# A two-layer graph network on one core: first loads on three queues, transposed score blocks in batch 0, wider score pieces, new instruction orders

## The chip, the cores and the metric

The kernel runs on one core of a Trainium2 chip. The core has five engines with an instruction queue each: TensorE (PE; its weight loads are listed as PEld), VectorE (DVE), ScalarE (ACT), GpSimd (POOL) and SyncE (SP), which here only starts transfers. Each engine runs its own instructions in their written order and waits for others at semaphores. SP, ACT and POOL can start DMAs. The metric is the device time of one execution in microseconds, the median of several.

## The reference

For each of 8 batches (x is 1024 x 128, adj 1024 x 1024 of zeros and ones), with EPS terms left out:

```python
def layer0(x, adj):                       # attention over the graph
    u = x @ x.T / sqrt(128)
    delta = softmax(u, -1) * adj
    att = delta / (delta.sum(-1) + 1e-10)
    ctx = triu(att, 1) @ (x @ Wl.T + bl) + diag(att) * (x @ Ws.T + bs) + tril(att, -1) @ (x @ Wr.T + br)
    return relu(ln_w * normed(ctx) + ln_b)

def layer1(x, adj):                       # graph convolution
    d = (adj.sum(-1) + 1e-5) ** -0.5
    return (d[:, None] * adj * d[None, :]) @ (x @ weight) + bias

x = layernorm(x + layer0(x, adj))
x = layernorm(x + layer1(x, adj))
```

## The kernel before

All work is in blocks of 128 rows; NB = 8 block rows a batch (called rows here), HB = 4 is half of them. The batches run one into the other: while batch b starts, the layer-1 products of batch b-1 (called p in the code) are still running. Nothing is scheduled by a tool at run time: for each engine the functions `first_batches`, `batch` and `last_batches` write out, call by call, the order of its work. The steps of a batch are:

- **x.** `load_x` brings all 8 rows of x; TensorE transposes them for batches 0 and 1 (`turn_x`), later ones are transposed by VectorE in 32 x 32 blocks and DMAs (`turn_rows`, `move_rows`). ScalarE writes the high part (`x_high`), VectorE the low part (`x_low`) of a split-precision product. `split_matmul` (L435) is three matmuls for one product.
- **Projections.** `project` multiplies one row by the three weights (384 columns) into the PSUM bank `ps_m`, and VectorE's `add_bias` moves it out. The orders place `m_read_h` ahead of the next projection, a wait until it has been moved.
- **Scores.** `scores(b, i)` makes 128 x 1024 scores of row i. Since x x' is symmetric, in batches 1 to 7 only the blocks from the diagonal on are multiplied, in one piece up to column 512 and one behind it; the blocks before the diagonal are transposed (L483) from copies that ScalarE made of earlier rows (`keep`, L841, into `kept`). In batch 0 (`halves(b)`) each row is multiplied in full, with rows 1 and 3 in the bank `ps_c`.
- **Softmax and mask.** VectorE's `row_max`, ScalarE's `exps`, VectorE's `masked` (times adjacency, with a sum).
- **Context.** TensorE turns the row (`turn_d`, 8 transposes), ScalarE moves it (`d_out`), GpSimd makes three masked copies of the diagonal block (`masks`), TensorE multiplies (`context_far`, `context_near`).
- **Norms.** `add_self`, `stats_c` (VectorE), `scale_c` (GpSimd: a power and a product), `norm_c` (ScalarE), `affine`, `stats_x`, `scale_x`, `norm_x`.
- **Layer 1.** The adjacency is transposed by VectorE (`turn_blocks`) and 16 DMAs for each half (`move_blocks`). `gather(b, i0, i1, j0, j1)` sums over source rows j for target rows i0 to i1; it waits until all of the group of rows that holds j1-1 have been normalised (`group_end`: rows 0 to 3, and in the last batch 4, 5 and 6, 7). `y_out` moves it out, `second_product` multiplies by the weight, `add_out` adds, `stats_f`, `scale_f` and `norm_f` normalise, `store` writes.

In the last batch the target rows are taken in three groups: 0 to 3, 4 to 6, and 7. Its normalisation is VectorE's, and all stores are on SP:

```python
            for i in range(i0, i1):                                   # norm_f_on, L286
                v = fin[:, i, :]
                last = eng.tensor_scalar(v, v, power["f"][:, i:i + 1], shift["f"][:, i:i + 1], ALU.mult, ALU.add)
```

Before the first transposes TensorE multiplies zeros (`first_products`), which VectorE writes into 512 columns first. The first loads all stand on SP: x, three weights, three biases broadcast to all partitions, then adjacency rows. Other engines' places that the text speaks of are the beginning and the end of each list.

## Time and profile before

| | us |
|---|---|
| three runs | 442.7, 443.6, 443.77 (median 443.6) |
| the profiled execution | 445.5 |
| its span, first to last instruction | 443.8 |
| TensorE busy | 431.7 (97%) |
| VectorE busy | 381.1 (86%) |
| ScalarE busy | 318.7 (72%) |
| GpSimd busy | 302.2 (68%) |

The engines' busy time says who is close to its limit over the whole; a busy time by stage says where. In the timeline, two starts on TensorE in a row tell the price of the first instruction better than its listed length, because matmuls overlap. A bracket behind a row gives the engine's idle time before it and what ended it.

### The profile page before, as it was taken

The numbers are of one execution on the slowest core, as the hardware profiler recorded it, in microseconds if no ns is written. First come the engines' busy times: TensorE is split into PE (matmuls) and PEld (weight loads), VectorE is DVE, ScalarE is ACT, GpSimd is POOL, SyncE is SP. The second block draws the span as 40 slices with busy tenths as digits, with TensorE's granted clock in tenths as the row PEclk, the third lists the DMA queues.
The fourth block names the chain that finished last, engine by engine and source line by source line (L and its number), as shares of the span: only waits on it lengthen the run. The fifth ranks groups of instructions, "written<-read, shape, count | busy, mean of one in ns | idle before, by whom it ended". The sixth has DMA issues, their size and how long they took to land. (4 is left out here: it accounts for less than half of the span.)

```text
span 443.8 us, 9076 instructions
## 1 busy us (share of the span) xinstructions
PE 431.7 (97%) x2775; PEld 355.7 (80%) x2775; DVE 381.1 (86%) x699; ACT 318.7 (72%) x674; POOL 302.2 (68%) x364
## 2 busy tenths in 40 slices
PE   7999999999999999999999999999999999999984
PEld 4789989779787888869887797977987789897743
DVE  2899898997999889997999989999799988998536
ACT  2588887778677787678876787677777777887420
POOL 2034666668777778758796687766877596897882
PEclk9999999999999999999999999999999999999998
DMA  5925859489765885468943888538866589254801
GB/s 163 350 68 146 264 162 258 143 214 257 151 185 136 246 244 136 153 168 280 220 141 111 204 273 216 178 110 216 267 137 189 142 245 273 55 132 98 199 19 54
DMA packets 68880, 79.91 MB, mean 180 GB/s; under 512 B 7232, under 2 KB 60608, under 8 KB 68832
## 3 DMA queue, kind: packets, MB, share of 16 engines
q1 hardware_dynamic: 68768, 79.26, 65.3%
q8 instruction: 23, 0.38, 0.4%
q14 instruction: 25, 0.20, 0.1%
q0 software_dynamic: 64, 0.07, 0.1%
HBM read 38.40 MB, written 4.19 MB: 96 GB/s over the span
## 5 line engine op out<-in xcount | busy, mean ns | idle before, releaser
L1481 POOL TENSOR_TENSOR dM<-dT,parts 128x384 f32<-128x384 f32 x64 | 72.5, 1132 | 67.4 <-ACT dT L851 54.9
L517 PE MATMUL ps_c<-h_sum,dT 128*128 128x128 f32 x896 | 110.4, 275 | 0.0
L517 PEld LDWEIGHTS ps_c<-h_sum,dT 128*128 128x128 f32 x896 | 106.4, 192 | 2.9 <-issue 2.5
L537 PE MATMUL ps_y<-aT,x1p 128*128 128x512 f32 x224 | 106.3, 593 | 0.0
L838 ACT ACTIVATE d_rows<-ps_u,nmax 128x1024 f32<-128x1024 f32 x62 | 68.8, 1110 | 49.4 <-DVE nmax L1124 49.3
L1124 DVE TENSOR_REDUCE nmax<-ps_u 128x1 f32<-128x1024 f32 x62 | 75.2, 1213 | 18.9 <-PE ps_u L483 16.9
L1131 DVE CUSTOM_DVE_ANT_0 d_rows<-d_rows,a_rows 128x1024 f32<-128x1024 f32 x64 | 83.7, 1315 | 0.3
L851 ACT ACTIVATE dT<-ps_d 128x1024 f32<-128x1024 f32 x64 | 65.4, 1022 | 25.7 <-PE ps_d L502 23.4
L1138 DVE STREAM_TRANSPOSE a_blk<-a_rows 128x1024 f32<-128x1024 f32 x64 | 77.7, 1228 | 0.0
L857 ACT ACTIVATE junk<-a_rows 128x1024 fp8e4<-128x1024 f32 x64 | 67.2, 1049 | 0.3
L502 PEld LDWEIGHTS ps_d<-parts,d_rows 128*128 128x128 f32 x512 | 58.9, 140 | 10.5 <-issue 9.8
L502 PE MATMUL ps_d<-parts,d_rows 128*128 128x128 f32 x512 | 66.3, 273 | 0.5 <-ACT dT L851 0.5
L537 PEld LDWEIGHTS ps_y<-aT,x1p 128*128 128x128 f32 x224 | 38.4, 191 | 24.4 <-issue 24.4
L437 PE MATMUL ps_u<-xT_hi 128*128 128x512 f32 (+3 forms) x96 | 43.1, 449 | 0.0
L298 DVE TENSOR_TENSOR h_sum<-ps_m,bias_bc 128x384 f32<-128x384 f32 x64 | 35.3, 552 | 6.9 <-PE ps_m L439 5.6
L523 PE MATMUL ps_c<-h_sum,dM 128*128 128x128 f32 x256 | 39.0, 275 | 0.0
L523 PEld LDWEIGHTS ps_c<-h_sum,dM 128*128 128x128 f32 x256 | 34.7, 191 | 3.3 <-issue 1.7
L438 PE MATMUL ps_u<-xT_lo,xT_hi 128*128 128x512 f32 (+3 forms) x96 | 34.0, 354 | 0.0
L439 PE MATMUL ps_u<-xT_hi,xT_lo 128*128 128x512 f32 (+3 forms) x96 | 33.9, 353 | 0.0
L1550 POOL TENSOR_TENSOR power_f<-var_f,minus_half 128x4 f32<-128x4 f32 (+2 forms) x17 | 21.9, 1290 | 17.3 <-DVE nmean_f L1237 14.8
L437 PE MATMUL ps_m<-wT_hi,xT_hi 128*128 128x384 f32 x64 | 29.5, 461 | 1.3 <-DVE h_sum L298 0.9
L872 ACT ACTIVATE c_rows<-c_rows,shift_c,power_c 128x128 f32<-128x128 f32 x64 | 26.3, 483 | 5.1 <-POOL shift_c L1501 5.1
(104 smaller groups left out, 751.6 us busy)
## 6 DMA issues: line engine op xcount, KB each, us to landing
a_rows<-in_adj_dram SPq DMA_DIRECT2D x64, 512.0 KB, 4.6
aT<-a_blk SPq DMA_DIRECT2D x224, 128.0 KB, 3.2
x_rows<-in_x_dram SPq DMA_DIRECT2D x8, 512.0 KB, 3.9
a_rows<-a_blk SPq DMA_DIRECT2D x32, 128.0 KB, 2.4
out_dram<-fin SPq DMA_DIRECT2D x15, 256.0 KB, 2.6
x_turned<-x_blk SPq DMA_DIRECT2D x96, 32.0 KB, 1.9
out_dram<-fin SPq DMA_DIRECT2D x1, 192.0 KB, 2.1
fin<-in_L_gnn_Wl_dram SPq DMA_DIRECT2D x1, 64.0 KB, 3.6
```

What stands on the lines that cost most here:

```text
L437: pe.matmul(o, hi_l, hi_r, start=True, stop=False)
L502: last = pe.transpose(ps_d[:, j, :], d_rows[:, g % 3, j * P:(j + 1) * P], ident)
L517: pe.matmul(ps_c[:, c_place(b, i), :], dT[:, i % 2, j, :], h_sum[:, b % 2, j, k * H:(k + 1) * H], start=t == 0, stop=False)
L523: last = pe.matmul(ps_c[:, c_place(b, i), :], dM[:, i % 2, k, :], h_sum[:, b % 2, i, k * H:(k + 1) * H], start=False, stop=k == 1)
L537: last = pe.matmul(y_bank(b, i0, i1), gathered(b)[:, j, :], turned(b)[:, i0:i1, :, j, :].rearrange("p i q c -> p (i q) c"), start=j == 0, ...
L838: act.activation(d_rows[:, g % 3, :], u_bank(b, i), ACT.Exp, bias=nmax[:, i % 2:i % 2 + 1], accum_out=zsum[:, i:i + 1]).then_inc(exp_done, 1)
L851: act.activation(dT[:, i % 2, :, :], ps_d[:, :, :], ACT.Copy).then_inc(dt_out, 1)
L857: act.activation(junk[:, :], a_rows[:, i, :], ACT.Copy, accum_out=deg[:, i:i + 1], saturate=False)\
L1124: dve.tensor_reduce(nmax[:, i % 2:i % 2 + 1], u_bank(b, i), AX.X, ALU.max, negate=True)\
L1131: dve.tensor_tensor_reduce(out=d_rows[:, g % 3, :], in0=d_rows[:, g % 3, :], in1=a_rows[:, i, :], scale=1.0, scalar=0.0, op0=ALU.mult, op1 ...
L1138: dve.transpose(a_blk[:, i, :, :, :], a_rows[:, i, :].rearrange("p (j m c) -> p m j c", m=NQ, c=Q))\
L1481: pool.tensor_tensor(dM[:, i % 2, :, :], dT[:, i % 2, i, :].rearrange("p (a c) -> p a c", a=1).to_broadcast([P, 3, P]), parts[:, :, :], AL ...
```

## The change

- `load_x_half`: batch 0's x comes in two loads with a semaphore each; the weights are loaded from ScalarE's queue, the biases and the norm constants from GpSimd's. GpSimd makes the identity first, and TensorE's start waits for it alone.
- The zeros are 128 columns, and the second warm-up product is 256 wide for 384.
- In batch 0, rows 0 to 3 are multiplied in full, the first half as soon as the first half of x is there; ScalarE keeps their right halves. Rows 4 to 7 are made as in the other batches, with transposes of kept blocks.
- `first_column`: rows 3 and 7 (from batch 1 on; row 7 in batch 0 too) multiply from one block further left, so that their short piece is 256 wide for 128, with one transpose less. Row 6 is not kept any more.
- Batch 0's odd projections go to the bank `ps_y`.
- The last normalisation subtracts the mean and multiplies by the power, without a shift, except where ScalarE does it: rows 0 to 6 of the last batch, whose rows 4 to 6 ScalarE also stores.
- All orders are new. In the last batch several gathers are cut into smaller steps.

```diff
+        def h_bank(b, j):
+            return (ps_y if b == 0 and j % 2 else ps_m)[:, 0:3 * H]
-        def halves(b):
-            return b == 0
+        def halves(b, i):
+            return b == 0 and i < HB
         def kept_before(b, i):
-            return (NB - 1) * (b - 1) + i
+            return (NB - 2) * b + min(i, NB - 2)
+        def first_column(i):
+            return i - (i % HB == HB - 1)
...
-            eng.wait_ge(f_scale, NB * b + i1)
+            eng.wait_ge(f_power, NB * b + i1)
             for i in range(i0, i1):
                 v = fin[:, i, :]
-                last = eng.tensor_scalar(v, v, power["f"][:, i:i + 1], shift["f"][:, i:i + 1], ALU.mult, ALU.add)
+                mean = f_stats_of(i, 1) if b == B - 1 and i >= NB - 2 else stats["f"][:, i, 1:2]
+                last = eng.tensor_scalar(v, v, mean, power["f"][:, i:i + 1], ALU.subtract, ALU.mult)
...
+            def load_x_half(b, half):
+                sp.dma_start(x_rows[:, b, blocks_of(half), :], x_block_rows(x, b, HALF * half, HALF * (half + 1)))\
+                  .then_inc(x_in[b] if half else x0_in, 16)
...
             def first_batches(b, p):
-                load_x(p)
-                load_weights()
-                load_biases()
+                load_x_half(p, 0)
+                load_x_half(p, 1)
                 load_a(p, 0)
-                load_a(p, 3)
                 load_a(p, 1)
...
-                for c in (slice(0, HALF), slice(HALF, HALF + 3 * P)):
-                    pe.matmul(ps_u[:, c], d_rows[:, 0, 0:P], d_rows[:, 0, 0:c.stop - c.start], start=True, stop=True)
+                zero = d_rows[:, 0, 0:P]
+                for n in (HB, 2):
+                    pe.matmul(ps_u[:, 0:n * P], zero, zero.rearrange("p (a c) -> p a c", a=1).to_broadcast([P, n, P]),
+                              start=True, stop=True)
...
             def scores(b, i):
-                pe.wait_ge(xt_split, 2 * (b + 1))
+                if b or i >= HB:
+                    pe.wait_ge(xt_split, 2 * (b + 1))
...
-                j0 = 0 if halves(b) else i
+                j0 = 0 if halves(b, i) else first_column(i)
                 for c in (slice(j0 * P, HALF), slice(max(j0 * P, HALF), N)):
+                    if b == 0 and i < HB:
+                        pe.wait_ge(xt_split, 2 if c.start else 1)
...
             def keep(b, i):
                 act.wait_ge(nmax_ready, NB * b + i + 1)
-                for v, j0, j1 in kept_parts(i):
-                    last = act.activation(v, ps_u[:, j0 * P:j1 * P].rearrange("p (j c) -> p j c", c=P), ACT.Copy)
+                for v, j0, j1 in kept_parts(i) if b or i else [(kept[:, 1, :, :], HB, NB)]:
+                    if b == 0 and j1 <= HB:
+                        continue
+                    last = act.activation(v, u_bank(b, i)[:, j0 * P:j1 * P].rearrange("p (j c) -> p j c", c=P), ACT.Copy)
...
-                gather(b, 0, HB, 0, HB)
-                gather(b, HB, NB - 1, 0, HB)
-                gather(b, NB - 1, NB, 0, 2)
-                gather(b, 0, HB, HB, NB)
+                gather(b, 0, HB, 0, 3)
+                gather(b, HB, NB - 1, 0, 1)
+                gather(b, 0, HB, 3, HB)
+                gather(b, HB, NB - 1, 1, HB)
+                gather(b, 0, HB, HB, NB - 2)
+                gather(b, 0, HB, NB - 2, NB)
```

VectorE's first instructions before (`nmax` is a row's maximum, `h_sum` a projection with its bias, `ISA d_rows,dsum` the masked product, `wT_lo` the low part of the weights):

```order
L1102 MEMSET d_rows 128x512
L1114 SCALAR_TENSOR_TENSOR xT_lo<-ps_m,xT_hi 128x512
L1106 SCALAR_TENSOR_TENSOR wT_lo<-ps_d,wT_hi 128x384
L1114 SCALAR_TENSOR_TENSOR xT_lo<-ps_y,xT_hi 128x512
L298 TENSOR_TENSOR h_sum<-ps_m,bias_bc 128x384
L1124 TENSOR_REDUCE nmax<-ps_u 128x1
L298 TENSOR_TENSOR h_sum<-ps_m,bias_bc 128x384
L1124 TENSOR_REDUCE nmax<-ps_c 128x1
L298 TENSOR_TENSOR h_sum<-ps_m,bias_bc 128x384
L1131 ISA d_rows,dsum<-d_rows,a_rows 128x1024
L1131 ISA dsum 128x1
```

and now:

```order
L1141 MEMSET d_rows 128x128
L1153 SCALAR_TENSOR_TENSOR xT_lo<-ps_m,xT_hi 128x512
L1153 SCALAR_TENSOR_TENSOR xT_lo<-ps_y,xT_hi 128x512
L1177 STREAM_TRANSPOSE a_blk<-a_rows 128x1024
L1163 TENSOR_REDUCE nmax<-ps_u 128x1
L1145 SCALAR_TENSOR_TENSOR wT_lo<-ps_d,wT_hi 128x384
L1163 TENSOR_REDUCE nmax<-ps_c 128x1
L311 TENSOR_TENSOR h_sum<-ps_m,bias_bc 128x384
L1170 ISA d_rows,dsum<-d_rows,a_rows 128x1024
L1170 ISA dsum 128x1
```

The first projection's bias has moved behind the maxima of rows 0 and 1, and block row 0 of the adjacency (`a_blk`) is turned ahead of them all.

TensorE's last instructions before, after the last context product (`ps_y` are the gathers for target rows 0 to 3, `ps_u` with 384 columns rows 4 to 6, with 128 row 7; `ps_m` and `ps_d` the second products):

```order
L537 MATMUL ps_y<-a_rows,h_sum 128x512 x4
L537 MATMUL ps_u<-a_rows,h_sum 128x384 x4
L537 MATMUL ps_u<-a_rows,h_sum 128x128 x2
L537 MATMUL ps_y<-a_rows,h_sum 128x512 x4
L537 MATMUL ps_u<-a_rows,h_sum 128x384 x2
L549 MATMUL ps_m<-w_sb,yT 128x128 x4
L537 MATMUL ps_u<-a_rows,h_sum 128x384 x2
L537 MATMUL ps_u<-a_rows,h_sum 128x128 x3
L549 MATMUL ps_d<-w_sb,kept 128x128 x3
L537 MATMUL ps_u<-a_rows,h_sum 128x128 x3
L549 MATMUL ps_d<-w_sb,kept 128x128
```

and now:

```order
L550 MATMUL ps_y<-a_rows,h_sum 128x512 x3
L550 MATMUL ps_u<-a_rows,h_sum 128x384
L550 MATMUL ps_y<-a_rows,h_sum 128x512
L550 MATMUL ps_u<-a_rows,h_sum 128x384 x3
L550 MATMUL ps_y<-a_rows,h_sum 128x512 x4
L550 MATMUL ps_u<-a_rows,h_sum 128x384 x2
L562 MATMUL ps_m<-w_sb,yT 128x128 x4
L550 MATMUL ps_u<-a_rows,h_sum 128x384 x2
L550 MATMUL ps_u<-a_rows,h_sum 128x128 x3
L562 MATMUL ps_d<-w_sb,kept 128x128 x3
L550 MATMUL ps_u<-a_rows,h_sum 128x128 x5
L562 MATMUL ps_d<-w_sb,kept 128x128
```

The gather into `ps_y` is cut after three, one and four steps (the four are two calls with a wait of their own each), and row 7's gather has moved behind the others.

VectorE's very last instructions before, from the sum of row 7 on:

```order
L1213 SCALAR_TENSOR_TENSOR fin<-ps_d,dinv,h_sum 128x128
L290 TENSOR_SCALAR fin<-fin,power_f,shift_f 128x128 x4
L1225 BN_STATS stats_odd<-fin 128x6
L1234 TENSOR_SCALAR var_f<-stats_odd 128x1
L1237 TENSOR_SCALAR nmean_f<-stats_odd 128x1
L290 TENSOR_SCALAR fin<-fin,power_f,shift_f 128x128 x4
```

and now:

```order
L1252 SCALAR_TENSOR_TENSOR fin<-ps_d,dinv,h_sum 128x128
L1264 BN_STATS stats_odd<-fin 128x6
L1273 TENSOR_SCALAR var_f<-stats_odd 128x1
L303 TENSOR_SCALAR fin<-fin,stats_odd,power_f 128x128
```

Seven normalisations have left VectorE's list, four of them from between the sum of row 7 and its statistics.

## Rows read from the trace of the kernel before

**Rows 1.** Busy time of each engine in one stage, its columns named above.

```profile
core 0: us, PE busy (x) PEld busy (x) DVE busy (x) ACT busy (x) POOL busy (x), PEclk, DMA share, GB/s
350.00:400.00 50.00, 50.00 (x349) 43.38 (x348) 45.46 (x84) 39.31 (x82) 39.64 (x45) 1.00 0.70 181
```

**Rows 2.** The timeline of the start: start, length, engine, line, what, [idle before].

```profile
1.51 3.35 PE L455 MATMUL ps_u<-d_rows 128*128 128x512 f32 x4 [1.51 <-DVE d_rows L1102]
...
4.27 4.93 SPq L315 DMA_DIRECT2D a_rows<-in_adj_dram  x6
...
4.81 1.09 PE L460 MATMUL ps_m<-parts,x_rows 128*128 128x128 f32 x4
...
6.56 0.69 DVE L1114 SCALAR_TENSOR_TENSOR xT_lo<-ps_m,xT_hi 128x512 fp32r<-128x512 f32 x1 [5.10 <-ACT xT_hi L830]
...
10.98 0.40 PE L439 MATMUL ps_u<-xT_hi,xT_lo 128*128 128x512 f32 x1
...
26.06 0.39 PE L437 MATMUL ps_u<-xT_hi 128*128 128x512 f32 x1
```

**Rows 3.** First 45 us: x's loads, their landing; then the adjacency loads' landing.

```profile
L308 SPq DMA_DIRECT2D x_rows<-in_x_dram x2: 441/552/664, 0.8 to 9.2; - x2
...
DMA to landing us min/median/max: 3.9/7.6/11.4
...
DMA to landing us min/median/max: 3.3/9.2/11.9
```

**Rows 4.** TensorE's timeline, a projection and row 2's scores of one batch.

```profile
109.11 0.33 PE L439 MATMUL ps_m<-wT_hi,xT_lo 128*128 128x384 f32 x1
109.28 0.28 PE L437 MATMUL ps_u<-xT_hi 128*128 128x256 f32 x1
...
109.64 0.40 PE L437 MATMUL ps_u<-xT_hi 128*128 128x512 f32 x1
109.87 0.40 PE L438 MATMUL ps_u<-xT_lo,xT_hi 128*128 128x512 f32 x1
```

**Rows 5.** TensorE's timeline, row 7's scores of one batch and what follows.

```profile
89.27 0.28 PE L438 MATMUL ps_u<-xT_lo,xT_hi 128*128 128x128 f32 x1
...
89.49 0.95 PE L483 MATMUL ps_u<-parts,kept 128*128 128x128 f32 x7
...
90.28 1.88 PE L537 MATMUL ps_y<-aT,x1p 128*128 128x512 f32 x4
```

**Rows 6.** Busy time from row 0's to row 4's maximum; then VectorE and ScalarE rows.

```profile
12.11:24.38 12.27, 11.09 (x58) 8.86 (x56) 11.60 (x17) 7.71 (x12) 1.78 (x1) 1.00 0.76 284
...
24.76 1.23 DVE L1138 STREAM_TRANSPOSE a_blk<-a_rows 128x1024 f32<-128x1024 f32 x1
...
95.33 1.64 ACT L872 ACTIVATE c_rows<-c_rows,shift_c,power_c 128x128 f32<-128x128 f32 x4
...
98.11 1.22 DVE L1124 TENSOR_REDUCE nmax<-ps_u 128x1 f32<-128x1024 f32 x1
...
100.00 1.11 ACT L838 ACTIVATE d_rows<-ps_u,nmax 128x1024 f32<-128x1024 f32 x1
...
101.09 0.92 ACT L844 ACTIVATE kept<-ps_u 128x896 f32<-128x896 f32 x1
```

**Rows 7.** The timeline of the end, all engines.

```profile
424.25 0.88 ACT L872 ACTIVATE h_sum<-c_rows,shift_x,scale_x 128x128 f32<-128x128 f32 x2 [2.09 <-POOL shift_x L1529]
...
427.54 3.67 PE L537 MATMUL ps_y<-a_rows,h_sum 128*128 128x512 f32 x8 [1.48 <-ACT h_sum L872]
...
437.29 0.49 PE L549 MATMUL ps_d<-w_sb,kept 128*128 128x128 f32 x2 [0.37 <-ACT kept L893]
...
438.26 0.34 DVE L1213 SCALAR_TENSOR_TENSOR fin<-ps_d,dinv,h_sum 128x128 f32<-128x128 f32 x1
438.51 1.13 DVE L290 TENSOR_SCALAR fin<-fin,power_f,shift_f 128x128 f32<-128x128 f32 x4
...
440.25 0.79 POOL L1550 TENSOR_TENSOR power_f<-var_f,minus_half 128x1 f32<-128x1 f32 x1 [0.69 <-DVE var_f L1234]
...
441.34 0.35 DVE L290 TENSOR_SCALAR fin<-fin,power_f,shift_f 128x128 f32<-128x128 f32 x1 [0.34 <-POOL shift_f L1554]
```

More of the change, by code:

```diff
@@ L273, in squares, with scaled_by_act @@
             return stats[norm][:, blk, 2]
+        def scaled_by_act(b, i1):
+            return b == B - 1 and i1 < NB
         def f_stats_of(i, t):
@@ L376, in first_batches, with batch @@
                 load_a(b, 0)
-                load_norm_constants()
+                load_a(b, 2)
+                move_blocks(p, 0)
+                load_a(b, 1)
+                load_a(b, 4)
+                move_blocks(p, 1)
+                load_a(b, 3)
+                load_a(b + 1, 0)
+                load_a(b, 7)
+                load_x(b + 1)
+                load_a(b, 6)
+                load_a(b, 5)
+                move_rows(b)
+            def batch(b, p):
                 load_a(b, 1)
@@ L379, in first_batches, with last_batches @@
                 move_blocks(p, 0)
+                load_a(b, 4)
+                load_a(b, 7)
+                load_a(b, 2)
+                move_blocks(p, 1)
+                store(p - 1, 0, HB)
+                load_a(b + 1, 0)
+                store(p - 1, HB, NB)
+                load_a(b, 3)
+                load_x(b + 1)
                 load_a(b, 6)
+                load_a(b, 5)
+                move_rows(b)
+            def last_batches(b, p):
                 load_a(b, 2)
+                load_a(b, 3)
+                load_a(b, 1)
+                move_blocks(p, 0)
+                load_a(b, 5)
+                load_a(b, 7)
+                store(p - 1, 0, HB)
@@ L490, in project @@
                     pe.wait_ge(const_ok, 1)
+                if b == 0 and j % 2:
+                    pe.wait_ge(xt_split, 2)
+                    wait(pe, h_added, j - 1)
                 s = slice(j * P, (j + 1) * P)
-                split_matmul(ps_m[:, 0:3 * H], xT_hi[:, b % 2, s], xT_lo[:, b % 2, s], wT_hi[:, :], wT_lo[:, :])\
+                split_matmul(h_bank(b, j), xT_hi[:, b % 2, s], xT_lo[:, b % 2, s], wT_hi[:, :], wT_lo[:, :])\
                     .then_inc(h_ready, 1)
@@ L817, in _, with load_weights @@
         def _(act):
+            def load_weights():
+                for k, w in enumerate((Wl, Wr, Ws)):
+                    act.dma_start(wraw[:, k, :], w).then_inc(const_in, 16)
             def weights():
@@ L886, in norm_x, with norm_f, store @@
                 normalize(gathered(b), c_rows, "x", i0, i1).then_inc(x1p_ready, i1 - i0)
+            def norm_f(b, i0, i1):
+                act.wait_ge(f_scale, i1)
+                act.wait_ge(f_norm, NB * b + i0)
+                normalize(fin, fin, "f", i0, i1).then_inc(f_norm, i1 - i0)
+            def store(b, i0, i1):
+                act.wait_ge(f_norm, NB * b + i1)
+                act.dma_start(x_block_rows(out, b, i0 * P, i1 * P), fin[:, i0:i1, :]).then_inc(fin_free[i0 // HB], 16)
             def y_out(b, i0, i1):
@@ L1088, in last_batches @@
                 y_out(b, NB - 1, NB)
+                norm_f(b, 0, HB)
+                norm_f(b, HB, NB - 1)
+                store(b, HB, NB - 1)
+            load_weights()
             first_batches(1, 0)
@@ L1380, in last_batches, with batch @@
+                row_max(b, 7)
+                masked(b, 6)
+                x_low(b + 1, 0)
+                stats_c(b, 0, HB)
+                stats_f(p, 0, HB)
+            def batch(b, p):
                 x_low(b, 1)
```

670 lines of the change are left out of this document (320 added, 350 removed).

## The prediction

> **What bounds the kernel now.** I read the busy time by stage first. In the stage from 350 us to 400 us TensorE is busy for all of the 50 us, VectorE for 45.5 (91%), ScalarE and GpSimd for 39 [rows 1]; the seven stages before it, back to 30 us, read alike for TensorE and VectorE. TensorE's starts follow one another without a hole there, so it is the bound in the middle, and a new order can take nothing from it: only less TensorE work can. Two other places are left. One is the start: work on TensorE begins at 4.81 us, and it limps until about 25 us [rows 2]. The other is the end: a wait of 1.48 us at 427.54 us, and 4 us of small steps behind the last matmul (start 437.29, end 437.78) [rows 7].
>
> To measure the start I use lost time: the moment at which an instruction starts, less the TensorE work that stands ahead of it at full rate. The full-rate steps from start to start are: a 512-wide split-precision matmul 0.23 us, a 384-wide one 0.17, a 256-wide one 0.12 (three from 109.28 to 109.64) [rows 4]; a 128-wide one 0.11 (two from 89.27 to 89.49), a 128x128 transpose 0.11 (seven from 89.49 to 90.28; I use 0.109) [rows 5]. Row 5's scores of batch 0 start at 26.06. Ahead of them stand 11 transposes (1.20), five rows of scores of six 512-wide matmuls (6.96), 8 projections of three 384-wide (4.16) and 3 turned rows of 8 transposes (2.62): 14.9 us. Lost so far: 11.1 us.
>
> **1. Less TensorE work.** Batch 0, rows 4 to 7: 24 wide matmuls become three 512-wide, three 384-wide and six 256-wide, with 21 transposes of kept blocks. That is -21 x 0.232 + 3 x 0.174 + 6 x 0.118 + 21 x 0.109 = -4.87 + 0.52 + 0.71 + 2.29 = -1.35 us. Rows 3 and 7 of batches 1 to 7: 42 matmuls go from 128 to 256 columns, at 0.12 for 0.11, +0.25 us; 14 transposes fall away, -1.53 us. Together **-2.6 us**, all on the path, since TensorE has no hole to hide it. Doubling the columns costs next to nothing only because the 128-wide product is as slow as the 256-wide one [rows 4, 5]. If the new 256-wide ones were priced by their width against the 128-wide, 42 x 0.11 = 4.6 us would come on top and the term would be +1.8; the row at 109.28 is the same operation in the same place, so I keep 0.12. ScalarE copies more for batch 0 (eight copies at most 0.9 us each [rows 6]) and less for every other batch; it is the emptier engine, and I take nothing for it beyond the chain below.
>
> **2. The start.** The warm-up products last 3.35 us, four passes of two products, at the lower rate [rows 2]. The second shrinks from 384 to 256 columns: 3.35 x 768/896 = 2.9, or less; and VectorE's memset is a quarter as wide, 0.3 us sooner. They end near 4.0 instead of 4.86; the memset's gain is my estimate, from 0.5 us that it can at most give. The first half of x is 256 KB; the whole landed 3.9 us after its issue at 0.8, at 4.7 [rows 3], so the half lands between 2.8 (half of 3.9 after the issue) and 4.7; I take 3.8. TensorE begins at 4.0. Eight transposes at 0.21 (1.09 for four [rows 2], the lower rate) end at 5.7. ScalarE's and VectorE's share of the first half ended 1.35 us after such transposes (5.90, then 6.56 + 0.69 = 7.25 [rows 2]); the first four end at 4.9, so the first half is there at 6.3 and the second, VectorE's 0.69 later, at 7.1. The six matmuls of row 0 run at the lower rate, 0.46 each: 6.3 to 9.0. Row 0's maximum starts at 9.0, where it started at 12.11 (the left end of the stretch in [rows 6]).
>
> From there VectorE's own queue is the chain up to row 4's maximum. Before, it was busy for 11.60 of the 12.27 us of this stretch, with five maxima, five bias additions and three masked products [rows 6]. The new order has the same between these points and one turned block row (1.23 [rows 6]) and the low part of the weights (at most the 0.69 of the wider one; I take 0.6) more. With 0.7 us of idle time, since row 1's scores come late, that is 14.1 us, and row 4's maximum ends at 23.1. Its exponentials (1.2) and kept copies (0.5) [rows 6] release row 5 at 24.8; the copies are new on this path. TensorE has by then 15.1 us of work behind it (four full rows 5.57, row 4 at 1.14, 15 transposes 1.64, projections 4.16, turned rows 2.62). Lost: 9.7 instead of 11.1, **-1.4 us**. The cover has to hold: after this point row 6's exponentials and copies have a context product of 3.5 us before them, and none of the later pairs is closer than 3.4 us of TensorE work.
>
> VectorE turns block row 0 before row 0's maximum, so it must have adjacency row 0 by 7.8 us. The issue was the eighth on SP, at 4.27 us [rows 2], the first at 0.8 [rows 3]: 0.5 us each. It is now the third, at 1.8. Loads of that kind took from 3.3 to 11.9 us [rows 3], the late ones behind others in line. In its own queue it has only x ahead of it now, so it should be nearer to x's own 3.9 than to the median of 9.2: I take 6 us, 7.8, just in time. At both ends it costs nothing or 2 us and more. The Trainium skill, page DMA: Bandwidth & Descriptors, section Issuing engines are not separate DMA queues, says that loads started on several engines still share the same 16 DMA engines and that only the issue time is saved; by that rule the three queues bring the 2.4 us of issue and no faster landing. No row here separates the two.
>
> **3. The end.** The wait at 427.54 is for the last two normalised rows, while rows 4 and 5 are ready since 425.13 (424.25 + 0.88) and the 512-wide gather asks for all four at once. Split, its two steps for rows 4 and 5 (2 x 0.86 us; eight passes last 3.67 less the drain, 0.43 each [rows 7]) fill the gap of 1.48; the other gathers moved there shift by one of 0.22. Left over 0.2 us: -1.3 us. Behind the last matmul VectorE adds up the last row at 438.26, half a microsecond late (busy with means), and normalises four finished rows (1.13 at 438.51) before that row's statistics and variance; these end 0.6 us later, when GpSimd's power starts at 440.25. Power and shift take until 441.34, and the last row is done at 441.69 [rows 7]: 3.9 us after the matmul. After: sum 0.34, statistics and variance 0.6, power 0.79 without a shift, row 0.35, with 0.3 us of handing over, 2.4 us. ScalarE normalises the other seven rows at 0.41 each (1.64 for four [rows 6]); three of them wait for GpSimd's power of rows 4 to 6, which ends 1.9 us after the second product of these rows as before, so ScalarE ends together with VectorE. -1.5 us. The store of three rows goes out beside the last one; I add 0.2 for its issue. The end gives **-2.6 us**.
>
> **4. The orders in the middle.** TensorE waits for nothing there now. The closest new spot is from row 0's scores to row 1's: the work between shrinks from 6.8 to 4.4 us (two projections, context 5, one turned row). Row 1 needs row 0's maximum 1.22, exponentials 1.11 and kept copies 0.92 [rows 6], 3.3 us with hand-overs. Before, the maximum (98.11), the exponentials (100.00) and the copies (101.09) of this row lay 2.9 us apart from first start to last, because VectorE had waited for the second product and ScalarE was behind with other rows; the second product now stands ahead of the scores. Slack 1.1 us, so nothing; ahead of it I allow 0.3 us for the whole middle (+0.3).
>
> The sum: 2.6 + 1.4 + 2.6 - 0.3 = 6.3 us. The profiled execution has a span of 443.8 us and took 445.5; after it, 437.5 and 439.2. The three runs' median is 443.6, so **437.3 us**.
>
> **The rivals.** A, the start gives nothing: adjacency row 0 lands at 1.8 + 8 us or later, VectorE stands behind it with row 0's maximum, and the 2 us pass on one for one; or TensorE's rate rises later than at 10.98 [rows 2], each matmul until then costing double. For it: that median of 9.2. Against: no broadcast loads ahead in the same queue. 437.3 + 1.4 = 438.7 us.
>
> B, waits come back in every batch, **slower than before**: the 4.4 us between rows 0 and 1 are too short. If ScalarE (the earlier rows' normalisation 1.64, a turned row 1.0, both in front) comes to the exponentials 2.6 us late, it passes the slack of 1.1 by 1.5, six times 1.5 = 9 us, and all later rows of the batch move with it: 446.3 us. It decides from 1.1 us of lateness; it is slower than before from 2.2. Against it: ScalarE is busy for 79% of the stage only [rows 1].
>
> C, the end gives half: GpSimd, which has the bias rows of batch 7 later in its order than before, holds back the sums, and ScalarE's three rows end after VectorE's: 437.3 + 1.3 = 438.6 us.
>
> D, better: the first half of x lands at 2.8 and the rate rises early, 1 us less at the start, and the 0.3 are not needed: 436.0 us.
>
> **How the numbers follow.** Forecast 0.55, A 0.17, B 0.10, C 0.08, D 0.10. The range takes in D with half a microsecond more at the end, and A and C together: 435.2 to 440.2. A measurement of this kernel can tell about 0.3% (1.3 us) from no change. Faster by more: all cases but B, less 0.02 for waits in the middle that eat most of the gain, 0.88. Of B's 0.10, 0.07 are slower, and 0.03, where the lateness is near 2.2 us, are within; with the 0.02 that makes 0.05.
>
> **What would show it.** TensorE's busy time falls by about 2.6 us while the stages from 60 to 400 us stay full. Right for the start: row 0's maximum near 9 us, row 5's scores near 24.8. Right for the end: the split gather starts without a wait for row 7's normalisation, and the last row is finished about 2.4 us after the last matmul. Wrong: a wait of TensorE for ScalarE's kept copies in each batch; a load of adjacency row 0 ahead of VectorE's second instruction group; ScalarE's last normalisation ending later than VectorE's.

## The result, and the profile after

| | before | after |
|---|---|---|
| median of six runs, us | 443.7 (442.7 to 445.0) | **450.8** (449.2 to 454.1) |
| profiled execution, us | 445.5 | 452.7 |
| its span, us | 443.8 | 450.9 |
| time behind the end of the last matmul, us | 6.0 | 6.8 |

The ratio is 1.0167 with an interval of 1.0124 to 1.0209. The prediction was 437.3 us, so it has the wrong sign. Busy time of the engines in the changed kernel's page:

```profile
PE 430.4 (95%) x2770; PEld 353.9 (78%) x2770; DVE 371.6 (82%) x677; ACT 322.8 (72%) x673; POOL 314.0 (70%) x355
```

TensorE has 1.3 us less of busy time and VectorE 9.5 us less; GpSimd has nine instructions fewer and 11.8 us more. TensorE's waits (what waits, what it waits for: us in total, times, longest), largest first:

```profile
PE ps_u L439 <- ACT kept L867: 7.6, 6, 1.5
PE ps_d L470 <- DMA fin<-in_L_gnn_Ws_dram: 2.6, 1, 2.6
```

Before, no scores waited for ScalarE's kept copies. The wait stands ahead of row 4's scores in batches 2 to 6 (five waits of 1.4 to 1.5 us, and one of 0.5 in batch 0). The chain behind one of them, in the timelines of GpSimd, ScalarE and TensorE (start, length, engine, what, [idle before]):

```profile
163.28 6.26 POOL L303 TENSOR_SCALAR fin<-fin,stats_f,power_f 128x128 f32<-128x128 f32 x8
169.51 1.03 POOL L1540 TENSOR_TENSOR power_c<-var_c,minus_half 128x4 f32<-128x4 f32 x1
...
170.91 1.65 ACT L895 ACTIVATE c_rows<-c_rows,shift_c,power_c 128x128 f32<-128x128 f32 x4 [1.83 <-POOL shift_c L1544]
172.46 1.09 ACT L859 ACTIVATE d_rows<-ps_u,nmax 128x1024 f32<-128x1024 f32 x1
...
174.27 0.47 PE L439 MATMUL ps_u<-xT_hi 128*128 128x512 f32 x1 [1.40 <-ACT kept L867]
```

Read it from below. TensorE waits for the kept copies of row 3. They stand behind row 3's exponentials (172.46), whose maximum VectorE had ready at 170.49. The exponentials stand behind ScalarE's norm of rows 4 to 7 of the batch before (170.91), which waited 1.83 us for GpSimd's shift. GpSimd computes it from statistics that VectorE had finished at 167.6; it was still busy, until 169.54, with eight last normalisations (`norm_f`). Those are the operation that the change rewrote. Grouped by line (busy us, mean ns of one), the changed kernel and then the one before:

```profile
L303 POOL TENSOR_SCALAR fin<-fin,stats_f,power_f 128x128 f32<-128x128 f32 x56 | 44.7, 810 | 0.2
```

```profile
L290 POOL TENSOR_SCALAR fin<-fin,power_f,shift_f 128x128 f32<-128x128 f32 x56 | 25.7, 471 | 0.1
```

The new form takes 810 ns for 471. Where the 7.1 us between the two spans lie, in lost time as the prediction defines it (start of an instruction less the TensorE work ahead of it at full rate):

| | predicted | profiled pair |
|---|---|---|
| TensorE work | -2.6 | -2.6 |
| start, up to row 5's scores of batch 0 | -1.4 | +1.1 |
| middle | +0.3 | +9.5 |
| gathers in the last batch, up to the last matmul | -1.3 | -1.7 |
| behind the last matmul | -1.3 | +0.8 |
| sum | -6.3 | +7.1 |

The middle can be read off from the repeating distance: the product of the adjacency (`ps_y<-aT,x1p`) starts at 110.75 us in one batch and at 164.67 in the next, 53.92 us; before it was 111.54 and 164.00, 52.46. Both profiles of this pair were slower than the median of their kernel (by 1.8 and 1.9 us), and the runs below show that most of it lies in the start.

### The profile page after: what moved, and what is told of

It is laid out like the page before. It is cut to its first block and busy times, and to the rows that moved or that the text cites. A ratio compares the mean times of both kernels' runs of the same rounds, so it can differ in the third digit from the quotient of the medians.

```text
span 450.9 us, 9021 instructions
## 1 busy us (share of the span) xinstructions
PE 430.4 (95%) x2770; PEld 353.9 (78%) x2770; DVE 371.6 (82%) x677; ACT 322.8 (72%) x673; POOL 314.0 (70%) x355
## 5 line engine op out<-in xcount | busy, mean ns | idle before, releaser
L550 PE MATMUL ps_y<-aT,x1p 128*128 128x512 f32 x224 | 104.9, 593 | 0.0
L874 ACT ACTIVATE dT<-ps_d 128x1024 f32<-128x1024 f32 x64 | 65.1, 1017 | 29.9 <-PE ps_d L514 16.2
L1170 DVE CUSTOM_DVE_ANT_0 d_rows<-d_rows,a_rows 128x1024 f32<-128x1024 f32 x64 | 79.4, 1246 | 0.2
L439 PE MATMUL ps_u<-xT_hi 128*128 128x256 f32 (+2 forms) x92 | 38.6, 420 | 8.5 <-ACT kept L867 7.6
L303 POOL TENSOR_SCALAR fin<-fin,stats_f,power_f 128x128 f32<-128x128 f32 x56 | 44.7, 810 | 0.2
L294 POOL TENSOR_TENSOR c_rows<-c_rows,lnw_bc 128x512 f32<-128x512 f32 x15 | 24.4, 1627 | 17.5 <-ACT c_rows L895 17.5
L311 DVE TENSOR_TENSOR h_sum<-ps_m,bias_bc 128x384 f32<-128x384 f32 x60 | 32.9, 548 | 1.8 <-PE ps_m L441 1.4
L1564 POOL TENSOR_TENSOR power_x<-var_x,minus_half 128x4 f32<-128x4 f32 (+1 forms) x17 | 22.3, 1310 | 15.8 <-DVE var_x L1240 15.8
L441 PE MATMUL ps_u<-xT_hi,xT_lo 128*128 128x256 f32 (+2 forms) x92 | 32.0, 348 | 0.0
```

Of the source, the lines that this page charges most:

```text
L303: last = eng.tensor_scalar(v, v, mean, power["f"][:, i:i + 1], ALU.subtract, ALU.mult)
L550: last = pe.matmul(y_bank(b, i0, i1), gathered(b)[:, j, :], turned(b)[:, i0:i1, :, j, :].rearrange("p i q c -> p (i q) c"), start=j == 0, ...
L874: act.activation(dT[:, i % 2, :, :], ps_d[:, :, :], ACT.Copy).then_inc(dt_out, 1)
L1170: dve.tensor_tensor_reduce(out=d_rows[:, g % 3, :], in0=d_rows[:, g % 3, :], in1=a_rows[:, i, :], scale=1.0, scalar=0.0, op0=ALU.mult, op1 ...
```

## Experiments

Each was compared with the kernel before on the same chip (443.6 to 443.9 us). "norm" is GpSimd's last normalisation, "period" the distance of two batches, "lost" the lost time at row 5's scores of batch 0.

| kernel | us | ratio to before, interval | norm, ns | period, us | lost, us |
|---|---|---|---|---|---|
| before (two profiles) | 443.7 | | 471, 468 | 52.46 | 11.1, 9.2 |
| after (two profiles) | 450.8 | 1.017, 1.012 to 1.021 | 810, 808 | 53.92, 53.90 | 12.2, 8.5 |
| n_shift | 440.3 | 0.992, 0.990 to 0.994 | 445 | 52.29 | 9.9 |
| n_addmul | 439.6 | 0.991, 0.988 to 0.994 | 459 | 52.29 | 8.5 |
| n_subc | 450.8 | 1.016, 1.014 to 1.018 | 807 | 53.91 | 8.6 |
| b_sub | 449.4 | 1.013, 1.010 to 1.016 | 877 | 53.48 | 9.5 |
| o_scale | 448.7 | 1.014, 1.009 to 1.019 | 812 | 53.90 | 8.7 |
| s_bcast | 439.3 | 0.991, 0.988 to 0.993 | 449 | 52.29 | 8.7 |
| s_sp | 445.1 | 1.003, 1.001 to 1.004 | 444 | 52.29 | 14.9 |
| s_order | 439.8 | 0.989, 0.985 to 0.993 | 446 | 52.29 | 9.9 |
| u_gather | 440.3 | 0.994, 0.993 to 0.996 | 459 | 52.29 | 8.9 |
| v_all | 438.0 | 0.988, 0.987 to 0.990 | 460 | 52.29 | 8.5 |

**n_shift: the form of the operation.**

```diff
-                last = eng.tensor_scalar(v, v, mean, power["f"][:, i:i + 1], ALU.subtract, ALU.mult)
+                if b < B - 1:
+                    last = eng.tensor_scalar(v, v, power["f"][:, i:i + 1], shift["f"][:, i:i + 1], ALU.mult, ALU.add)
...
```

The rest of the edit brings back VectorE's negated mean and GpSimd's shift, without which this form can't be computed.

> The changed kernel, in which GpSimd's and ScalarE's last normalisation of batches 0 to 6 is a multiplication by the power and an addition of the shift again (with VectorE's negated means and GpSimd's shift, as before); batch 7 keeps the changed form. All orders stay. Theory 1, the form of the operation: the subtract-and-multiply form takes 810 ns on GpSimd where multiply-and-add took 471 (28.6 us busy for 44.7 would follow), and eight in a row put ScalarE late for row 3's exponentials. Then the five waits of TensorE for the kept copies ahead of row 4's scores (1.4 to 1.6 us each, 7.6 us together) vanish, and the time is about 450.8 - 8 = 443 us, 440 if the lateness at the end goes with them. Theory 2, the orders: the distance from row 3's to row 4's scores is too short whatever the form costs; the waits stay above 1 us each and the time stays at 450 us.

440.3 us, with every order of the changed kernel in place. The five waits are gone; the first three rows of TensorE's waits are all from the start:

```profile
PE ps_u L460 <- DVE d_rows L1143: 1.1, 1, 1.1
PE ps_m L466 <- DMA x_rows<-in_x_dram: 0.5, 1, 0.5
PE ps_u L441 <- ACT kept L869: 0.5, 1, 0.5
```

In GpSimd's timeline the eight normalisations take 3.45 us for 6.26, and now GpSimd waits for VectorE's statistics, not the other way round:

```profile
159.58 3.45 POOL L303 TENSOR_SCALAR fin<-fin,power_f,shift_f 128x128 f32<-128x128 f32 x8
163.54 1.01 POOL L1542 TENSOR_TENSOR power_c<-var_c,minus_half 128x4 f32<-128x4 f32 x1 [0.52 <-DVE nmean_c L1224]
```

So 10.5 us, the whole way from 450.8 to 440.3, hang on the form of one operation. The rival, that the new orders are too tight whatever the form costs, has fallen.

**n_addmul and n_subc: which part of the form.** Both read the mean from a tile with one column for each row; they differ in the operation and in the sign.

```diff
-                last = eng.tensor_scalar(v, v, mean, power["f"][:, i:i + 1], ALU.subtract, ALU.mult)
+                last = eng.tensor_scalar(v, v, nmean["f"][:, i:i + 1], power["f"][:, i:i + 1], ALU.add, ALU.mult)       # n_addmul
+                last = eng.tensor_scalar(v, v, nmean["f"][:, i:i + 1], power["f"][:, i:i + 1], ALU.subtract, ALU.mult)  # n_subc
...
```

The tile `nmean` holds the negated mean in n_addmul and the mean itself in n_subc.

> The changed kernel, in which GpSimd's last normalisation of batches 0 to 6 is written as an addition of the negated mean and a multiplication by the power, both from tiles with one column for each row; it computes the same with no shift. Theory 1a, the price lies in the subtraction or in the mean read from the statistics tile (stride of three): an operation falls from 810 to about 470 ns, the waits ahead of row 4's scores go, about 442 us. Theory 1b, the price lies in the multiplication standing second: it stays at 810 ns, the waits stay, 450 us.

> The changed kernel, in which GpSimd's last normalisation of batches 0 to 6 stays a subtraction and a multiplication, but reads the mean from a tile with one column for each row (VectorE copies it there); it differs from the run with the addition (n_addmul, 459 ns an operation, 439.6 us) in the sign and in the operation alone. Theory O, the operation subtract is dear on GpSimd: an operation takes some 810 ns, the waits ahead of row 4's scores are back, about 450 us. Theory M, the mean's place is dear (in the changed kernel it is column 1 of three in the statistics tile): about 460 ns and 440 us.

```profile
L305 POOL TENSOR_SCALAR fin<-fin,nmean_f,power_f 128x128 f32<-128x128 f32 x56 | 25.0, 459 | 0.2
```

```profile
L305 POOL TENSOR_SCALAR fin<-fin,nmean_f,power_f 128x128 f32<-128x128 f32 x56 | 44.5, 807 | 0.2
```

The first row is n_addmul's, the second n_subc's: the same line, operands, shapes and count. Neither the place of the mean nor the multiplication in second place matters. The subtraction alone costs 350 ns (the medians say the same, 443 and 792), and with it the waits and the 450.8 us are back:

```profile
PE ps_u L443 <- ACT kept L871: 7.6, 6, 1.6
```

The Trainium skill, page GPSIMD Engine Reference, section 3.1 Elementwise — side-by-side cycle accounting, gives an elementwise operation about 1.8 cycles an element at best and about 2.6 with two tensor inputs; it has no price for a subtraction. These runs show one: 459 against 807 ns for equal operands.

**b_sub: the same part alone, in the kernel before.**

```diff
-                last = eng.tensor_scalar(v, v, power["f"][:, i:i + 1], shift["f"][:, i:i + 1], ALU.mult, ALU.add)
+                if b < B - 1:
+                    last = eng.tensor_scalar(v, v, stats["f"][:, i, 1:2], power["f"][:, i:i + 1], ALU.subtract, ALU.mult)
```

> The kernel before with one part of the change alone: GpSimd's last normalisation of batches 0 to 6 in the subtract-and-multiply form, without negated means and shift. All orders are those of before. Theory 1: the operation takes 810 ns instead of 471 (48 of them, 16 us more on GpSimd); what it costs in time depends on the slack of the old orders: between 0 and 9 us slower, and I expect some 3 us, 447 us. Theory 2, the orders alone make the loss: the operation is as dear but the time stays at 443.7 within 1 us.

449.4 us, 5.7 more than before. The old orders have more room than the new ones (1.0 us a batch is lost, not 1.6), but a wait comes up at another place, ahead of a projection, because VectorE is late with a bias; and the wait at the end is longer than it was (1.9 us for 1.5):

```profile
PE ps_m L443 <- DVE h_sum L304: 4.0, 6, 0.8
PE ps_y L543 <- ACT h_sum L878: 1.9, 1, 1.9
```

Why VectorE is late stands in the timelines of one such place:

```profile
160.95 2.05 DVE L1137 CUSTOM_DVE_ANT_0 d_rows<-d_rows,a_rows 128x1024 f32<-128x1024 f32 x1
...
161.91 4.09 POOL L294 TENSOR_SCALAR fin<-fin,stats_f,power_f 128x128 f32<-128x128 f32 x4
...
163.53 0.44 PE L443 MATMUL ps_m<-wT_hi,xT_hi 128*128 128x384 f32 x1 [0.78 <-DVE h_sum L304]
```

VectorE's masked product takes 2.05 us where the one before it took 1.21, while four of GpSimd's normalisations, which overlap it, take 4.09 us where the four before them took 3.13. The bias behind it, for which TensorE waits 0.78 us, starts only at 162.93. So the two engines seem to hold each other up where their work overlaps; no run tests this. It also raises the operation's mean here to 877 ns, with the median at 792 as in the other kernels. At the end, after the longer wait, TensorE's granted clock is at the lower level from 431 to 434.4 us (windows: span, busy, instructions, granted clock, DMA share, GB/s):

```profile
432.00:434.00 2.00, 2.00 (x3) 0.50 0.00 0
```

From the first gather to the last matmul it takes 19.9 us for 17.9: 0.4 of wait and 1.7 of clock. My 3 us were too little (the operations are 56, not the 48 of my text). My rival, that the form costs nothing in the old orders, has fallen.

**o_scale: does the place or the sum of GpSimd's work harm?**

```diff
                 norm_f(p - 1, 0, HB)
+                scale_c(p, HB, NB)
                 norm_f(p - 1, HB, NB)
-                scale_c(p, HB, NB)
```

> The changed kernel with the slow operation kept (subtract and multiply, 808 ns) and one step of GpSimd's order moved, in batches 2 to 6: the scale and shift of rows 4 to 7's first norm stand behind four of the eight normalisations instead of behind all eight. Theory 1 in full (the price of the operation harms through its place: eight of them, 6.3 us, stand ahead of the power for which ScalarE waits before row 3's exponentials): GpSimd can start that power some 2 us earlier, when VectorE's statistics are there (167.4 us instead of 169.5 in the batch shown), the waits of 1.4 to 1.6 us ahead of row 4's scores fall to under 0.5 us, and the time is 443 to 446 us. Rival, GpSimd as a whole is too busy in this stage (the sum of its work harms, not the place): the wait moves to another row's kept copies or to a bias row, and the time stays at 450 us.

448.7 us: the rival was right. The wait ahead of row 4's scores is gone, and five others have come:

```profile
PE ps_y L550 <- ACT x1p L895: 6.5, 5, 1.3
```

GpSimd's timeline from the moved step to the shift for which these wait:

```profile
163.96 1.03 POOL L1540 TENSOR_TENSOR power_c<-var_c,minus_half 128x4 f32<-128x4 f32 x1 [1.09 <-DVE nmean_c L1222]
165.12 0.20 POOL L1544 TENSOR_TENSOR shift_c<-power_c,nmean_c 128x4 f32<-128x4 f32 x1
165.30 3.14 POOL L303 TENSOR_SCALAR fin<-fin,stats_f,power_f 128x128 f32<-128x128 f32 x4
168.40 1.00 POOL L1524 TENSOR_TENSOR dM<-dT,parts 128x384 f32<-128x384 f32 x1
169.36 2.25 POOL L294 TENSOR_TENSOR c_rows<-c_rows,lnw_bc 128x512 f32<-128x512 f32 x1
171.76 1.28 POOL L296 TENSOR_TENSOR c_rows<-c_rows,lnb_bc 128x512 f32<-128x512 f32 x1
172.99 1.01 POOL L1524 TENSOR_TENSOR dM<-dT,parts 128x384 f32<-128x384 f32 x1
173.96 0.68 POOL L1556 TENSOR_SCALAR vdeg<-deg 128x4 f32<-128x4 f32 x1
174.72 1.04 POOL L1558 TENSOR_TENSOR dinv<-vdeg,minus_half 128x4 f32<-128x4 f32 x1
175.76 1.96 POOL L1564 TENSOR_TENSOR power_x<-var_x,minus_half 128x4 f32<-128x4 f32 x1
177.84 0.20 POOL L1568 TENSOR_TENSOR scale_x<-power_x,dinv 128x4 f32<-128x4 f32 x1
178.18 0.20 POOL L1572 TENSOR_TENSOR shift_x<-scale_x,nmean_x 128x4 f32<-128x4 f32 x1
```

Not one row behind the first carries a bracket: from 163.96 to 178.38 us GpSimd never waits, and TensorE's product starts at 180.21 after 1.33 us of waiting. GpSimd is the bound of this stretch, at 70% of busy time over the whole. The period is 53.90 us as without the edit; a step moved forward only passes the same lateness on to the next one who waits.

**after2 and before2: how far the start varies.** Both kernels once more, unchanged.

> The changed kernel once more, for a second look at its start. In the first profile the third weights load came late (TensorE waited 2.6 us at 11.0 us) and adjacency row 0 landed at 9.76 us; in the profiles of n_shift and n_addmul, whose first 25 us are the same instructions, neither wait was there and row 5's scores began at 24.98 and 23.59 us instead of 27.26. If that is chance of a single execution, the second profile has row 5's scores of batch 0 anywhere from 23.5 to 27.5 us, and its five waits of 1.4 to 1.6 us ahead of row 4's scores are the same as in the first. If it belongs to the changed form of the normalisation, row 5's scores stand at 27.3 again.

> The kernel before once more, for a second look at its start. Its first profile has row 5's scores of batch 0 at 26.06 us and 11.1 us of lost time. The run b_sub, with the same first 25 us of instructions, lost 9.4 us there, because TensorE's rate rose earlier. If the start varies from execution to execution, the lost time lies between 9.4 and 11.2 us; the rest of the batches keeps its 52.46 us a batch.

Row 5's scores of batch 0 start at 27.26 us in the first profile of the changed kernel and at 23.65 in the second; before, at 26.06 [rows 2] and 24.13:

```profile
27.26 0.41 PE L439 MATMUL ps_u<-xT_hi 128*128 128x384 f32 x1
```

```profile
23.65 0.41 PE L439 MATMUL ps_u<-xT_hi 128*128 128x384 f32 x1
```

```profile
24.13 0.45 PE L437 MATMUL ps_u<-xT_hi 128*128 128x512 f32 x1
```

So a single profile's start is uncertain by 2 to 3.6 us; the batches behind it repeat (periods of 53.90 and 52.43 us in the second profiles). In the first profile of the changed kernel the last piece of the third weights load came at 10.96 us (at 6.9 in the second), adjacency row 0 at 9.76 (6.75):

```profile
9.78 1.25 DVE L1177 STREAM_TRANSPOSE a_blk<-a_rows 128x1024 f32<-128x1024 f32 x1 [2.48 <-DMA a_rows<-in_adj_dram]
...
11.00 0.55 PE L470 MATMUL ps_d<-parts,fin 128*128 128x128 f32 x3 [2.59 <-DMA fin<-in_L_gnn_Ws_dram]
```

and the wait was followed by a slow stretch (span, busy, instructions, granted clock, DMA share, GB/s):

```profile
8.00:10.00 2.00, 0.41 (x2) 1.00 1.00 267
10.00:12.00 2.00, 1.00 (x6) 1.00 1.17 291
12.00:14.00 2.00, 2.00 (x7) 0.50 1.14 173
```

TensorE was nearly idle from 8.4 to 11 us, and then its granted clock stood at the lower level, 1.2 GHz, until some 15 us, with 512-wide steps of 0.43 us. The second profile has 1.00 throughout. Seven profiles with the changed start (both of after, n_shift, n_addmul, n_subc, o_scale, u_gather) lose 12.2, 8.5, 9.9, 8.5, 8.6, 8.7 and 8.9 us, 9.3 on average; three with the old one (both of before, b_sub) lose 11.1, 9.2 and 9.5, 9.9 on average. The 9.2 of before2 are just below the 9.4 that I gave as the lower end.

A late load is not the only thing that varies. In n_shift adjacency row 0 was there at 6.91 us, but the first scores went at the lower rate until 9.4 us, 0.43 us from start to start, where the second profile of the changed kernel has 0.23 from 7.02 us on:

```profile
7.65 0.63 PE L442 MATMUL ps_u<-xT_lo,xT_hi 128*128 128x512 f32 x1
8.08 0.63 PE L443 MATMUL ps_u<-xT_hi,xT_lo 128*128 128x512 f32 x1
```

The column of the granted clock has 1.00 for this stretch too, so here the rate has to be read from the starts. The same holds for the two profiles before: scores at 10.05 and 10.55 us are 0.5 us apart in the first, while the second steps by 0.23 from 8.75 us on.

**s_sp, s_order and s_bcast: three queues or the order of the loads.** All from n_shift. s_sp has everything on SyncE's queue in the order x, weights, biases, adjacency row 0; s_order moves one call; s_bcast keeps the weights on ScalarE's queue and takes the broadcasts from GpSimd's. Core of the edits:

```diff
                 load_x_half(p, 0)
                 load_x_half(p, 1)
                 load_a(p, 0)                        # s_order and s_bcast, as in n_shift; in s_sp it stands below the biases
+                for k, w in enumerate((Wl, Wr, Ws)):        # s_sp and s_order
+                    sp.dma_start(wraw[:, k, :], w).then_inc(const_in, 16)
+                for k, v in enumerate((bl, br, bs)):
+                    sp.dma_start(bias_bc[:, k * H:(k + 1) * H], v.partition_broadcast(P)).then_inc(bias_in, 16)
...
```

The same loads leave the other queues, and the norm constants go to SyncE's queue further down.

> The run n_shift (440.3 us) with all first loads on SyncE's queue again, in the order x, weights, biases, adjacency row 0, as before the change; the two halves of x and all the rest of the start's order stay. Theory Q1, three queues bring issue time only, and what they bring is taken back by broadcasts that slow the others' packets: adjacency row 0 lands at about 9 to 12 us (issued at 4.7 instead of 1.83), VectorE's turning of it waits 1 to 3 us, and the time is 1 to 3 us above n_shift's, 442 us. Theory Q2, the queue doesn't matter, since the same bytes stand ahead: within 1 us of n_shift's.

> The run s_sp (all first loads on SyncE's queue, 445.1 us) with one change of order: adjacency row 0 is issued straight behind x, ahead of the weights and the biases. Theory O, the order is what counts: in s_sp adjacency row 0 was issued at 4.75 us and landed at 12.5, 7.8 us later, because three weights and three broadcast biases stood ahead of it in its queue; issued at 1.83 it lands at about 7 us as with three queues (6.6 to 7.0 us in four profiles), the weights some 1 us later than with a queue of their own (8 us), and the time is 440.3 us as n_shift's, within 1 us. Theory Q, separate queues are what counts: the one queue carries too much, adjacency row 0 or the weights land at 9 us or later, and the time is 442 us or more.

> The run with multiply-and-add (n_shift), in which the broadcast loads of the biases and of the norm constants are issued on SyncE's queue, behind adjacency row 0, instead of on GpSimd's. Theory S1, the broadcasts on GpSimd's queue hold back the weights and adjacency row 0 (their 4096-byte packets took 0.39 to 1.9 us for 0.16): weights land by 8 us instead of 10.96, adjacency row 0 by 8 us instead of 9.76, the wait of 2.6 us at 11.0 goes, and the time is 2 us less than n_shift's. Theory S2, the DMA engines are filled by bytes and it doesn't matter whose queue they come from: the landings move by under 1 us, and the time stays within 1 us of n_shift's.

s_sp loses 4.8 us against n_shift, more than its first theory said. VectorE waits 5.62 us for adjacency row 0; TensorE waits 5.8 us, from 9.7 us on, for the weights' low part, which VectorE makes behind it, and loses its rate (windows as above):

```profile
12.53 1.25 DVE L1180 STREAM_TRANSPOSE a_blk<-a_rows 128x1024 f32<-128x1024 f32 x1 [5.62 <-DMA a_rows<-in_adj_dram]
```

```profile
12.00:14.00 2.00, 0.00 (x0) 0.50 1.04 424
14.00:16.00 2.00, 0.51 (x2) 0.50 1.01 414
16.00:20.00 4.00, 4.00 (x15) 0.66 1.09 364
```

s_order, the same single queue with one call moved, is at 439.8 us; its wait is 0.38:

```profile
7.59 1.25 DVE L1180 STREAM_TRANSPOSE a_blk<-a_rows 128x1024 f32<-128x1024 f32 x1 [0.38 <-DMA a_rows<-in_adj_dram]
```

So the order of the loads is worth 5.3 us here, and the two further queues nothing that these runs can tell (440.3 against 439.8). The rule of the Trainium skill that the prediction named (page DMA: Bandwidth & Descriptors, section Issuing engines are not separate DMA queues: several issuing engines save issue time only) is borne out: on the one queue of s_order the third weights load was issued 1.5 us later than in n_shift (3.32 for 1.84) and landed 1.3 us later (8.4 for 7.08). s_bcast's 1.0 us against n_shift is no difference, since the two intervals overlap; its loads landed no sooner (third weights 7.07 us for 7.08, adjacency row 0 6.86 for 6.91). Its theory S1, that broadcasts on GpSimd's queue hold the others back, is not shown.

**u_gather: the split gather.** From n_addmul:

```diff
-                gather(b, 0, HB, HB, NB - 2)
-                gather(b, 0, HB, NB - 2, NB)
+                gather(b, 0, HB, HB, NB)
```

> The run n_addmul (439.6 us) with the split of the gather undone: rows 0 to 3's gather takes block rows 4 to 7 in one step again. If the split gives what the prediction said, TensorE waits again for ScalarE's last two normalised rows, by 1.3 to 1.5 us at about 421 us, and the time is 1.3 us more, 440.9 us. If ScalarE's rows are early in this kernel anyway, there is no wait and no change.

```profile
422.50 1.96 PE L554 MATMUL ps_y<-a_rows,h_sum 128*128 128x512 f32 x4 [1.49 <-ACT h_sum L898]
```

The wait of [rows 7] (1.48 us) is back with 1.49. From the first of these gathers to the last matmul, a stretch that the start does not reach, it takes 17.9 us for 16.2 in n_addmul, 1.7 more. In the profiles' spans it is 2.0 us more, 0.4 of them at the start, and in the medians 0.7, which is inside the scatter of the start.

**v_all: the fastest version.** n_addmul with the loads of s_bcast (the second layer's weights too), and row 6's last normalisation on VectorE:

```diff
-                norm_f(b, HB, NB - 1)               # ScalarE
+                norm_f(b, HB, NB - 2)
...
                 stats_f(b, NB - 1, NB)              # VectorE
+                norm_f(b, NB - 2, NB - 1)
                 norm_f(b, NB - 1, NB)
```

> An attempt at the fastest version. From the changed kernel: the normalisation as addition and multiplication (as n_addmul, 439.6 us), biases, norm constants and the second layer's weights on SyncE's queue behind adjacency row 0 (as s_bcast), and in batch 7 row 6's last normalisation on VectorE, in the 0.8 us in which it waits for row 7's power, instead of as ScalarE's third row. At the end ScalarE's rows ended at 435.49 us, 3.0 us behind the last matmul, and VectorE's at 435.09; with two rows instead of three they end together at 435.1: 0.4 us less. The start gives 0 to 1 us. Expected 438.7 us, between 438.0 and 439.5. If the end is set by the landing of ScalarE's store and not by its rows, the 0.4 us aren't there.

438.0 us, 1.2% faster than before. The rows at its end:

```profile
432.23 0.37 DVE L307 TENSOR_SCALAR fin<-fin,stats_odd,power_f 128x128 f32<-128x128 f32 x1
...
432.56 0.88 ACT L906 ACTIVATE fin<-fin,shift_f,power_f 128x128 f32<-128x128 f32 x2 [0.37 <-POOL shift_f L1605]
433.06 0.34 DVE L307 TENSOR_SCALAR fin<-fin,stats_odd,power_f 128x128 f32<-128x128 f32 x1 [0.46 <-POOL power_f L1599]
```

The engines end together, at 433.44 and 433.40. Behind the last matmul (end 431.14) there are 5.1 us, for 5.4 in n_addmul and 5.7 in n_shift. What each of the three edits gives was not measured apart.

## Why the prediction was wrong, point by point

**Left out: the rewritten normalisation.** The failed step is no term of the sum but one that is missing from it. The prediction spoke of "power 0.79 without a shift" at the end and nowhere asked what subtract-and-multiply costs on GpSimd, where 56 of these operations are. The trace of before had no row for it; it had to be bounded from both sides, and 0 was taken without a word. It measures +350 ns each. The change of form brings all of +10.5 us (n_shift), on a kernel that would otherwise have been 0.8% faster: 440.3 us for 443.7, still 3.0 above the forecast of 437.3.

**Step 4, the middle (+0.3).** It measured +9.5. The five batches with the wait are 1.63 us longer than in n_shift, 8.2 together; 1.1 more are lost in the last batch, where TensorE waits twice for GpSimd's masked copies (0.3 us each, at 376 and 394 us). The prediction named a wait for ScalarE's kept copies as what would show it wrong, and rival B had the kind of failure (waits in every batch, 9 us, 446.3 us) at a chance of 0.10. But B's place (rows 0 to 1) and its cause (ScalarE's own load) were wrong. It was row 3 to row 4, and ScalarE was late because GpSimd was. I had followed ScalarE's queue alone, and not its norm back to GpSimd's power. Without the slow form the middle is as predicted: the period falls by 52.46 - 52.29 = 0.17 us.

**Step 1, less TensorE work (-2.6): right.** Seven periods at 0.17 are the 1.2 us of rows 3 and 7 (1.53 less 0.25 predicted). Doubling the short piece cost next to nothing. TensorE's busy time is 429.9 us in the second profile before and 427.6 in n_addmul, 2.3 less; in the first pair it was only 1.3, because stretches at the lower rate count as busy time. Batch 0's own 1.35 are not measured apart.

**Step 2, the start (-1.4): not shown, and wrong in its base.** Adjacency row 0 had to land by 7.8 us and does so at 6.6 to 7.0 in six of seven profiles. The predicted lost time of 9.7 is met by the average of 9.3. But the 11.1 us it was subtracted from belonged to one execution with a slow start; two more profiles of that start have 9.2 and 9.5. The averages differ by 9.9 - 9.3 = 0.6 us, with three profiles against seven that scatter by 3.7, so these runs show no gain for certain. The prediction's "445.5 against a median of 443.6" was the sign of it: 1.9 us by which the profiled execution was unusual, which I subtracted from the time but left in the term. Rival A (a late load, 1 to 2 us lost) did occur, in the first profile of the changed kernel, as chance and not as rule; its second half, a rate that rises late, is what n_shift has. The prediction had put row 0's scores at the lower rate, 0.46 us each; in six of the seven profiles they go at 0.23, so that the 9.7 fit 9.3 partly by luck.

**Step 3, the end (-2.6).** The split gather is right: no wait, -1.7 by lost time, and 1.49 us of wait when undone. Behind the last matmul I predicted 1.5 - 0.2 = 1.3 less. n_shift, which has the form of batch 7 unchanged, has 0.3 less: VectorE's last row is done 2.6 us behind the matmul (2.4 predicted), but ScalarE's three rows end at 3.0 (rival C's second half), and from the last store's issue to the end of the span it takes 2.7 us for 2.1; the store carries three rows where it was one, but no run tests whether that is the cause. In the changed kernel itself the term is +0.8: two more groups of four slow normalisations on GpSimd (3.14 us each for 1.75) push the bias rows back, for which VectorE waits:

```profile
435.11 3.14 POOL L303 TENSOR_SCALAR fin<-fin,stats_f,power_f 128x128 f32<-128x128 f32 x4
...
440.76 1.13 DVE L1252 SCALAR_TENSOR_TENSOR fin<-ps_m,dinv,h_sum 128x128 f32<-128x128 f32 x4 [8.14 <-POOL h_sum L1587]
```

That sum starts 440.76 - 439.24 = 1.5 us behind the end of its product, and the later ones follow it. Rival C had named GpSimd's bias rows for this.

**What is left without the subtraction.** The spans of n_shift and of the first profile before (438.2 and 443.8 us) differ by 5.6 us, close to the 6.3 predicted, but by luck: that first profile had the slow start. By medians it is 3.4 us (440.3 for 443.7). The second profile before is near its median (443.3 us), as n_shift's is (440.0). Between these two, TensorE work gives -2.6; the start +0.7 where -1.4 was predicted; the middle +0.5 for +0.3; the gathers -1.7 for -1.3; the end -0.3 for -1.3. Of the 2.9 us that are missing, 2.1 lie at the start and 1.0 at the end.

## What to carry to other kernels

Every rewritten operation gets a price on the engine on which it runs, also when it looks like an algebraic equal of the old one; when the trace has no row of that form, its bounds go into the range. When an engine waits on a chain over three engines, follow the chain back to the one with no idle time in that stretch, whatever its share over the whole; moving a step there only moves the wait. And a start that is read from one profile needs a second one before a microsecond is taken from it.

## What the runs showed of the hardware that I had not expected

- On GpSimd a subtraction in a two-step operation of 128 x 128 float32 with per-partition operands takes 807 ns where the addition with the same operands takes 459 (n_subc, n_addmul), and multiply-and-add 444 to 471. Why is open. On VectorE the subtract form takes 0.35 us for one row (447.43 in the changed kernel), as the other form did [rows 7].
- After 2.6 us of near idleness at 8.4 us TensorE's granted clock was at the lower level until about 15 us; in s_sp it fell during a wait of 5.8 us and stayed there until between 18 and 19 us. There a late load at the start is paid twice.
- The landing of the same loads, issued at the same times, varied by 3 to 4 us between two executions (adjacency row 0 at 6.75 and 9.76 us, the third weights load at 6.9 and 10.96). What delayed them in one execution is open.
